# The inverse norms' way through DRAM in fewer, larger transfers, and a new table of places

## What is computed

```python
def l2norm(t):
    return t / jnp.maximum(jnp.linalg.norm(t, axis=-1, keepdims=True), 1e-12)
...
qkv = x @ Wqkv
q, k, v = (sh(q), sh(k), sh(v))          # 16 heads of 64
q = l2norm(q) * qs
k = l2norm(k) * ksc
q = q * cos * scale + rotate_half(q) * sin * scale
k = k * cos * inv + rotate_half(k) * sin * inv
out = local_attention(q, k, v)           # windows of 32 with a look back of one
...
for i in range(DEPTH):                   # 6
    x = attn_layer(shift_tokens(x), ...) + x
    x = ffn_layer(shift_tokens(x), ...) + x
```

## Time and profile before

| what | value |
|---|---|
| median of 3 executions | 3387.93 us (3386.78 to 3393.01) |
| the profiled execution: its time | 3385.34 us |
| its span (first to last instruction) | 3383.5 us |
| mean granted TensorE clock | 0.983 of full speed |
| busy in the span | TensorE 94%, its weight loads 57%, VectorE 71%, ScalarE 76%, GpSimd 65% |

### The profile page before, as it was taken

How to read it: one execution, slowest core, us unless ns; L and a number is a source line. 1 busy time by engine, 2 the same in 40 slices (tenths; PEclk the granted TensorE clock), 3 DMA queues, 4 the chain that set the end, 5 groups by cost and what they waited for, 6 DMA issues and landing times.

```text
span 3383.5 us, 125778 instructions
## 1 busy us (share of the span) xinstructions
PE 3179.4 (94%) x52744; PEld 1944.9 (57%) x52744; DVE 2411.4 (71%) x2940; ACT 2557.1 (76%) x5866; POOL 2216.2 (65%) x2135
## 2 busy tenths in 40 slices
PE   7999996899999999999999999999999999999996
PEld 3444442566666666666666666666666666656653
DVE  3656654677777777777777777777777777777773
ACT  5666663687877878887778887878787888788884
POOL 0000003877788777788777887778887778877771
PEclk9999997899999999999999999999999999999998
DMA  3232322444445444554444544444544454544441
GB/s 112 76 81 72 80 71 72 161 157 147 156 154 165 151 152 152 162 162 161 149 152 155 167 157 158 148 155 157 167 153 158 150 162 158 160 149 157 149 141 40
DMA packets 290260, 472.26 MB, mean 140 GB/s; under 512 B 90398, under 2 KB 128540, under 8 KB 289564
## 3 DMA queue, kind: packets, MB, share of 16 engines
q1 hardware_dynamic: 263376, 447.69, 41.6%
q10 hardware_dynamic: 26316, 16.52, 1.7%
HBM read 124.21 MB, written 7.34 MB: 39 GB/s over the span
## 4 chain that ended last, share of the span: by engine, by line
PE 56%; DVE 10%; ACT 8%; SPq 8%; POOL 7%; issue 5%; DMA 5%; POOLq 0%; ACTq 0%; DVEq 0%
PE PS L542 56%; DMA RB<-root_scratch 4%; POOL K L1314 2%; DVE TPB L938 2%; DVE H L990 2%; SPq L528 2%; ACT SC L1227 2%; SPq L499 2%; POOL Q L1332 2%; ACT SX L1203 1%; ACT H L1263 1%; SPq L531 1%; SPq L507 1%; SPq L517 1%; ACT AOT L1240 1%
## 5 line engine op out<-in xcount | busy, mean ns | idle before, releaser
L938 DVE SCALAR_TENSOR_TENSOR TPB<-PS,VEC,C 128x1024 f32<-128x1024 f32 x768 | 970.8, 1275 | 413.4 <-ACT SX L1203 400.6
L1227 ACT ACTIVATE SC<-PS,BQ,RQ 128x64 f32<-128x64 f32 x3072 | 964.0, 431 | 2.8 <-POOL BQ L1350 2.7
L1203 ACT ACTIVATE SX<-PS 128x512 f32<-128x512 f32 x768 | 461.8, 614 | 282.8 <-PE PS L542 282.0
L1314 POOL TENSOR_TENSOR K<-K,RB 128x512 f32<-128x512 f32 x384 | 492.8, 1283 | 153.9 <-DMA RB<-root_scratch 148.3
L1332 POOL TENSOR_TENSOR K<-TPB,TR 128x512 f32<-128x512 f32 x384 | 494.6, 1288 | 0.0
L1332 POOL TENSOR_TENSOR Q<-TPB,TR 128x512 f32<-128x512 f32 x384 | 493.1, 1284 | 0.0
L542 PE MATMUL PS<-LXH,LH 128*128 128x512 f32 x768 | 403.8, 526 | 49.6 <-DVE TPB L938 34.0
L1358 POOL TENSOR_TENSOR SC<-SC,RC 128x1024 f32<-128x1024 f32 x192 | 366.3, 1908 | 29.4 <-DVE RC L961 29.1
L542 PE MATMUL PS<-AOT,LO 128*128 128x512 f32 x768 | 370.0, 605 | 0.0
L542 PEld LDWEIGHTS PS<-PP,VV 64*64 64x64 f32 x12288 | 271.8, 133 | 154.6 <-issue 152.6
L542 PE MATMUL PS<-PP,VV 64*64 64x96 f32 (+1 forms) x12288 | 340.5, 246 | 1.9 <-issue 0.8
(11 more groups left out here) (169 smaller groups left out, 5672.9 us busy)
## 6 DMA issues: line engine op xcount, KB each, us to landing
TR<-TPB SPq DMA_DIRECT2D x768, 256.0 KB, 3.0
RB<-root_scratch SPq DMA_DIRECT2D x768, 128.0 KB, 3.0
PP<-PX SPq DMA_DIRECT2D x1344, 64.0 KB, 2.0
WS<-in_wqkv ACTq DMA_DIRECT2D x72, 128.0 KB, 2.7
PP<-PX SPq DMA_DIRECT2D x192, 48.0 KB, 2.0
QA<-TH SPq DMA_DIRECT2D x128, 64.0 KB, 2.1
QA<-TL SPq DMA_DIRECT2D x128, 64.0 KB, 2.1
KA<-TH SPq DMA_DIRECT2D x128, 64.0 KB, 2.1
```

What stands on the lines that cost most here:

```text
L938: e.scalar_tensor_tensor(TPB[:, n % 3:4 + n % 2:3 + n % 2 - n % 3, w, :], g, VEC[:, l, 9 + w:10 + w], C[:, at:at + 1024].rearrange("p (o c ...
L1203: e.activation(SX[i % 3][:, :], bk("PJ", key)[:, :], ACT.Square).then_inc(sem["pj_act"], 1)
L1227: p = e.activation(SC[m % 2][:, g, :, :].rearrange("p x k -> p (x k)"), bank[s][:, at:at + 64], ACT.Exp, bias=BQ[m % 2][:, g:g + 1], scale ...
L1314: e.tensor_tensor(dst, dst, RB[n % 2][:, :], ALU.mult).then_inc(sem["pr_pool"], 1)
```

## The change

RW becomes one transfer of all 128 rows (a new DRAM layout) instead of four of 16 rows. RB is done for two head pairs at a time, into one buffer that holds both: two transfers of 64 x 4 pieces of 256 numbers (256 KB each) instead of four of 64 x 512 (128 KB each). It waits for both PR of the two head pairs before, where it used to wait for the PR two head pairs back. SyncE issues 58 transfers a unit. The scratch in SBUF is as large as before. All numbers of `PLACE` are new (F3 and RB stand for them here). All else is the same.

```diff
-    "AD": -5.818, "NM1": -3.383, "NM2": -3.485, "RW": -3.172, "RQ": -1.687, "RB": -2.851, "PR": -2.077, "XS": -8.031,
...
-    "F2n": 14.367, "F3": 14.678, "F3l": 14.708, "TB": (15.846, 16.303), "F4": (15.887, 16.123, 16.178), "F5": 17.130,
...
+    "AD": -5.851, "NM1": -3.402, "NM2": -2.875, "RW": -4.010, "RQ": -1.986, "RB": -3.718, "PR": -2.307, "XS": -8.125,
...
+    "F2n": 14.439, "F3": 14.960, "F3l": 15.105, "TB": (15.933, 16.247), "F4": (15.944, 16.141, 16.217), "F5": 17.160,
...
-        lay(n + P["RB"], o.put, "RB", n)
         lay(n + P["PR"], o.put, "PR", n)
...
-            for st in ("S1", "MX", "BQ", "SU", "NP", "TT", "PX", "PVn"):
+            for st in ("RB", "S1", "MX", "BQ", "SU", "NP", "TT", "PX", "PVn"):
...
-        rootd = nc.dram_tensor("root_scratch", (2, 16, L), F32, kind="Internal").ap()
+        rootd = nc.dram_tensor("root_scratch", (2, 128, 128), F32, kind="Internal").ap()
...
-        RB = [sb(f"RB{i}", [128, L]) for i in range(2)]
+        RB = sb("RB", [128, 4, 2, 128])
...
                 elif st == "RW":
                     q, = key
                     if q > 1:
-                        for n in (4 * q - 6, 4 * q - 5):
-                            on.wait_ge(f"rb_in{n % 2}", 32 * (n // 2) + 32)
+                        for i in range(2):
+                            on.wait_ge(f"rb_in{i}", 32 * q - 32)
                     on.wait_ge("nm_pool", 4 * q + 4)
-                    for c in range(4):
-                        e.dma_start(rootd[q % 2, :, 128 * c:128 * c + 128], NV[32 * c:32 * c + 16, 2, :]).then_inc(sem[f"rr_in{q % 2}"], 16)
+                    e.dma_start(rootd[q % 2], NV[:, 2, :]).then_inc(sem[f"rr_in{q % 2}"], 16)
                 elif st == "RB":
-                    n, = key
-                    q = n // 4
-                    if n > 1:
-                        on.wait_ge("pr_pool", n - 1)
-                    on.wait_ge(f"rr_in{q % 2}", 64 * (q // 2) + 64)
-                    at = 8 + 4 * (n % 4 // 2) + n % 2
+                    p, = key
+                    q = p // 2
+                    if p:
+                        on.wait_ge("pr_pool", 2 * p)
+                    on.wait_ge(f"rr_in{q % 2}", 16 * (q // 2) + 16)
                     for s in range(2):
-                        r = rootd[q % 2, at + 2 * s:at + 2 * s + 1, :]
-                        e.dma_start(RB[n % 2][64 * s:64 * s + 64, :], r.broadcast_to([64, L])).then_inc(sem[f"rb_in{n % 2}"], 16)
+                        at = 8 + 4 * (p % 2) + 2 * s
+                        r = rootd[q % 2].rearrange("(o c r) k -> o c (r k)", o=1, c=4)[:, :, 128 * at:128 * at + 256]
+                        e.dma_start(RB[64 * s:64 * s + 64, :, :, :].rearrange("p c e k -> p c (e k)"),
+                                    r.broadcast_to([64, 4, 256])).then_inc(sem[f"rb_in{p % 2}"], 16)
...
-                    on.wait_ge(f"rb_in{n % 2}", 32 * (n // 2) + 32)
-                    e.tensor_tensor(dst, dst, RB[n % 2][:, :], ALU.mult).then_inc(sem["pr_pool"], 1)
+                    p = n // 2
+                    on.wait_ge(f"rb_in{p % 2}", 32 * (p // 2) + 32)
+                    e.tensor_tensor(dst.rearrange("p (c k) -> p c k", c=4), dst.rearrange("p (c k) -> p c k", c=4), RB[:, :, n % 2, :],
+                                    ALU.mult).then_inc(sem["pr_pool"], 1)
```

More of the change, by code:

```diff
@@ L1206, in scalar_program @@
                     if q:
-                        on.wait_ge(f"rr_in{(q - 1) % 2}", 64 * ((q - 1) // 2) + 64)
+                        on.wait_ge(f"rr_in{(q - 1) % 2}", 16 * ((q - 1) // 2) + 16)
                         on.wait_ge("rq_pe", q)
```

## The result

| | us | |
|---|---|---|
| the kernel before | 3390.78 | median of 6 (3386.78 to 3394.24) |
| the change | 3687.73 | median of 6 (3673.76 to 3700.02) |
| ratio | 1.0873 | 95% interval 1.0847 to 1.0899 |

The change costs 297 us where I forecast a gain of 28. Its profiled execution (3673.76 us) shows where. First the page's head: span and busy time of each engine, of the change and then the same two lines of before.

A forecast was written before the change was run, and what follows sets the result against it. TensorE, busy 2458.11 of 2550.00 us, was taken as the bound. 48 units x 0.28 = 13.4 us plus 14.5 us of PR waits made 28 us off 3385.3; with 2.6 us to the median, 3360 us, range 3345 to 3373.

The forecast's parts named there:

- Its landing is now that of 256 KB ... I take 3.8, being the nearer in size.: RB's landing after issue: between 3.0 us as now and 3.8 of another 256 KB DRAM scratch read; 3.8 taken.
- RB's data late: RB lands over 1.3 us later than 3.8, so S1 waits for PR: 24 us slower, 3412 us; chance 0.05.
- the signs that I had named for "wrong": Waits for XCL at F4's start, for RB at a pair not a quad's first, or TensorE waiting at new spots.
- Why small descriptors are slow (HBM only): Fixed 3 cycles a packet on top of 32 for 1 KB, 64 for 2 KB: RB's pieces 4% dearer.
- The TS behind RB feed an AD that comes only after the next pair's first PR.: SyncE's queue: TS transfers behind RB are needed only late, so RB's waiting there was given no cost.
- 14 issues fewer "at nothing": SyncE issues 14 fewer transfers a unit, some 8 us; counted as no gain.
- F3's new place: F3 behind both PT ahead of S1: PJ, S1 and F4 start 0.55 us later in the clean unit.
- the term for F4: From F4's start to the next PJ, waits vanish: 5.8 us forecast in place of 6.58.
- net 0.28 us a unit: PJ behind F4 starts at about 2127.7 in place of 2127.98; over 48 units 13.4 us gained.
- only the waits for PR go: Loss before S1 and gain in F4 cancel, leaving 14.5 us gained: 3373 us; chance 0.17.
- XS ahead of the table load: On ScalarE, second Gelu ends near 2125.2, so the sixth F4 group starts at 2125.9, not 2126.02.
- What is gained here should stay gained, and what is lost too.: TensorE stands only from VP ahead of S1 to the PJ behind F4, so changes there carry through; no size given.

The follow-up runs named there:

- e10: The change with the table of places of before and RB reading each partition's own row: 3387 us, ratio 0.9991 to 1.0011.
- e4: The change with the table of places of before, RB's shared 1 KB pieces still 16 KB apart: 3551 us, ratio 1.0459 to 1.0523.
- e6: The change, new places included, with RB reading each partition's own row instead of shared roots: 3411 us, ratio 1.0040 to 1.0083.
- e2: The kernel before with each row RB reads split into two pieces of 1 KB: 3393 us, ratio 1.0009 to 1.0029.
- e8: The kernel before with only RB moved, directly behind RW in SyncE's order: 3417.86 us, ratio 1.0079 to 1.0105.
- e15: The change with the places of before and RB cut into eight transfers of 16 partitions: 3548.57 us, ratio 1.0448 to 1.0487.
- e17: As e15, with four copies of the roots written, one for each 16 partitions: 3754.49 us, ratio 1.1056 to 1.1096.
- e9: The kernel before with only F3 and F3l at the change's places: 3375.34 us, ratio 0.9944 to 0.9974.
- e12: As e9, with XS also put ahead of the table load: 3372.00 us, ratio 0.9941 to 0.9964.
- e3: The kernel before with the new table of places alone, transfers as before: 3418 us, ratio 1.0076 to 1.0153.

## Why the prediction was wrong, point by point

- **"Its landing is now that of 256 KB ... I take 3.8, being the nearer in size."** This term failed. The row that I borrowed is a read that nobody shares, and e10 shows it right for such a read (4.0). The change's read lands after 5.6 to 5.8 us. With the same places, own rows take away 164 us (e4 to e10) or 275 us (change to e6).
- **The rival "RB's data late".** Its place was right and its bound too (1.3 us later than 3.8; it came 2.0 later). Its price of 24 us was wrong: it counted only S1's wait for PR. In the change TensorE has no such wait in its list; TS and PX, behind the reads in SyncE's queue, land late, and the waits appear at PT and PV. Two of the signs that I had named for "wrong" came: TensorE stands at PV, where it hardly stood (69.4 us for 1.9), and GpSimd waits 60 us for RB at the second two head pairs of the quads (22 before). Part of the price is then the clock: the change's busy time rose by 87 us for the same matmuls.
- **The rule in the Trainium skill, "DMA: Bandwidth & Descriptors", "Why small descriptors are slow (HBM only)",** under which this rival "would not come about". Runs agree where pieces aren't shared: 512 of 1 KB cost nothing (e10). Shared halves for one head pair cost the kernel 0.2% (e2), and RB lands in 3.2 us for 3.0, near the rule's 4%. For 64 readers on pieces 16 KB apart the trace doesn't agree: 5.6 us (e4) for 4.0 (e10).
- **"The TS behind RB feed an AD that comes only after the next pair's first PR."** This step failed too. It asked who waits for the transfer's data and forgot who waits for its source to be free: PT two head pairs on. In e8 that costs 32 us, more than the whole forecast gain of 28. RB did go out sooner, 1.59 us after RW in the unit shown (1.8 in the median of the change) in place of 3.26; I had 2.0.
- **14 issues fewer "at nothing"**: right at the old places (e10). What more issues cost isn't shown: e15 has 24 more than e4 and the same time, and e17 changes more than their number.
- **F3's new place.** The sign was right; the term for F4 was too large. In the unit shown, 2121.30 - 2115.32 = 5.98 us remain from F4 to the PJ behind it, of 6.58 (forecast 5.8). VP and PJ ahead of S1 wait 0.42 + 0.68 = 1.10 us in place of 0.26 + 0.23 = 0.49. The means over 41 units of both traces agree: this stretch takes 6.09 us in place of 6.69, and all the rest of a unit 50.73 in place of 50.44, although the waits for PR in it, 14.5 us or 0.30 a unit, are gone but for one of 0.5 us. So some 0.6 us a unit are lost ahead of S1 (forecast 0.55) and 0.6 won in F4 (forecast 0.83), and of **"net 0.28 us a unit"** next to nothing is left. What stays is about what the waits for PR were: 3388.7 - 14.5 = 3374.2, and e9 measured 3375.3. That is my rival "only the waits for PR go", with the transfers left alone.
- **XS ahead of the table load**: nothing that can be told from e9 (e12).
- **"What is gained here should stay gained, and what is lost too."** The second half came true: a unit takes 63.1 us in the change in place of 57.1 (means of 41 units). The premise, that TensorE is not seen to stand elsewhere in a unit, did not hold for the change: 69.4 us of its standing are at PV.

The costs do not add up: the new table costs 31 us with the old transfers and 132 (297 - 165) with the new. In it the slow reads stand ahead of two head pairs' TS at once, with RW's landing in front. And SyncE's standing at RB for both PR, which holds up all behind it, is 163 us in the change, 51 in e6 (new places, own rows) and 25 in e4 (old places). How much of the 132 us each of these makes was not tried.

Open: why pieces 16 KB apart and shared are so much slower than either alone. The runs show the place in DRAM to be part of it, not what is contended there, and a number of readers between 4 and 64 was not separated from the number of issues. e3 also doesn't split into e8 and e9 (+32 and -13 would make 3406; e3 measured 3418, with one of its four executions at 3445); the places that make up the rest weren't tried.

## What to carry to other kernels

In this kernel a transfer's price was not set by its bytes and pieces alone: where many partitions read one small piece of DRAM, borrow no price from a read of distinct addresses, and try another distance between the pieces before giving the layout up. In a queue that issues in order, ask of every transfer behind a slower one both who waits for its data and who waits to overwrite its source. Merging transfers saved nothing here (e10); in the kernel before, SyncE's listed waits came to 369 of 2550 us, so it had time to spare. Moving one consumer (F3) behind two others did help.

## What the runs showed of the hardware

- At the old places, 512 pieces of 1 KB in two transfers land in 4.0 us when each partition reads its own, 4.4 when each address has 4 readers and all lie 16 KB apart, 4.3 to 4.4 with 64 readers at other distances, and 5.6 with 64 readers and 16 KB between pieces. The last costs the kernel 165 us of 3387, the others 1 to 65.
- Transfers queued behind the slow reads land later too, though TR reads and writes SBUF alone: with the shared reads in place of own rows TR went from 2.8 us (e10) to 4.1 (e4) at the old places, and from 4.1 (e6) to 5.7 (change) at the new.
- The DMA share of time hardly shows it, since the kernel gets longer with it (0.52 in e4 and e10); the median to landing does (5.6 and 4.0 us).
- TensorE's granted clock fell where it stood often: 0.983 over the span with 204 us of standing, 0.950 with 405. These are two levels mixed over a span (2.4 GHz is 1.00 and 1.2 GHz half of it). Behind the wait of 4.36 us shown above the next 3.50 us had 0.58, so that wait cost more than its own length.
